# Routed feed forward in pairs of slot tiles, with a direct scatter of the last batch

## What is computed

```python
x = x + attn_a(_layernorm(x))      # 8 heads of 128, relative positions
x = x + ffn(_layernorm(x))
x = x + attn_b(_layernorm(x))      # 16 heads of 8, one shared key head, causal
x = x + ffn(_layernorm(x))
# ffn
gate_scores = softmax(x @ Wg.T)
topk_val, topk_idx = top_k(gate_scores, 2)       # shares then sum to one
for e in range(8):
    h = x @ W1[e].T + b1[e]                      # 512 columns
    a, b = split(h, 2)
    out = out + ((a * sigmoid(b)) @ Wo.T + bo) * comb[..., e:e + 1]
```

## Time and profile before

| | us |
|---|---|
| median of 3 runs | 2738.0 |
| the profiled execution, as timed | 2737.45 |
| its span in the trace | 2735.7 |
| mean granted TensorE clock (share of full speed) | 0.939 |
| first feed forward's slot tiles, first to last matmul | about 1601 to 1732 |
| end of the opening of the second attention | about 1831 |
| second feed forward, first matmul to the end | about 2544 to 2736 |

### The profile page before, as it was taken

The page is one execution under the profiler, slowest core; times in us unless marked ns, Lnnn a source line. Parts: engine busy times, 40 slices in busy tenths (PEclk is TensorE's granted clock), DMA queues, the critical chain, the costliest instruction groups (busy, mean ns, idle before and its releaser), DMA issues.

```text
span 2735.7 us, 42920 instructions
## 1 busy us (share of the span) xinstructions
PE 2468.2 (90%) x13784; PEld 1930.7 (71%) x13784; DVE 1875.9 (69%) x4952; ACT 1566.4 (57%) x3189; POOL 452.5 (17%) x827
## 2 busy tenths in 40 slices
PE   4999898999999999999999977789988988888686
PEld 3788787888888888888888865565555554554565
DVE  4677775676767778767776655578777877773464
ACT  3566665666666566666666634436657656656242
POOL 1000012000000021000110005341212223334145
PEclk7999999999999999999999989679999999999795
DMA  3665568555555566565666526310000000000264
GB/s 115 216 223 209 179 242 284 180 206 208 209 208 207 188 224 223 202 216 181 218 217 222 205 65 189 96 35 1 1 1 1 1 1 16 9 22 11 82 204 122
DMA packets 153109, 385.66 MB, mean 141 GB/s; under 512 B 17972, under 2 KB 74932, under 8 KB 152564
## 3 DMA queue, kind: packets, MB, share of 16 engines
q1 hardware_dynamic: 137562, 345.74, 36.6%
q0 software_dynamic: 12208, 35.62, 4.2%
q10 hardware_dynamic: 3120, 1.57, 0.2%
HBM read 192.02 MB, written 193.53 MB: 141 GB/s over the span
## 4 chain that ended last, share of the span: by engine, by line
PE 75%; DVE 12%; ACT 4%; issue 4%; DMA 2%; POOL 1%; another core or an unknown queue 1%; SPq 0%; ACTq 0%; DVEq 0%; POOLq 0%
PE ps L305 8%; PE ps L307 8%; PE ps L306 8%; PE ps L854 7%; PE ps L959 5%; PE ps L921 5%; PE ps L829 5%; PE ps L828 5%; PE ps L867 4%; PE ps L941 4%; PE ps L869 4%; PE ps L868 4%; DVE ps L1603 2%; ACT r_P L1177 1%; PE ps L743 1%
## 5 line engine op out<-in xcount | busy, mean ns | idle before, releaser
L1129 ACT ACTIVATE a_Ph<-ps 128x512 fp32r<-128x512 f32 x512 | 305.5, 597 | 469.1 <-PE ps L854 469.1
L1177 ACT ACTIVATE r_P<-ps 128x512 f32<-128x512 f32 (+3 forms) x768 | 330.5, 492 | 213.0 <-PE ps L941 192.8
L1520 DVE CUSTOM_DVE_ANT_0 a_sp<-ps,a_sp 128x1024 f32<-128x1024 f32 x256 | 313.2, 1223 | 180.6 <-PE ps L307 160.9
L1526 DVE TENSOR_TENSOR a_Pl<-ps,a_Ph 128x512 fp32r<-128x512 f32 x512 | 349.1, 682 | 10.0 <-ACT a_Ph L1129 10.0
L828 PE MATMUL ps<-a_fa,a_ua 128*128 128x384 f32 (+2 forms) x960 | 329.6, 355 | 27.5 <-ACT a_rt L1114 14.6
L1122 ACT ACTIVATE a_sp<-a_sp,a_nm 128x1024 f32<-128x1024 f32 x256 | 295.0, 1152 | 44.6 <-DVE a_nm L1520 43.9
L854 PE MATMUL ps<-ident,a_sp 128*128 128x128 f32 x2048 | 309.8, 274 | 0.0
L921 PE MATMUL ps<-r_K,r_Q 128*128 128x512 f32 (+3 forms) x768 | 283.9, 403 | 23.2 <-DVE r_mx L1603 13.3
L854 PEld LDWEIGHTS ps<-ident,a_sp 128*128 128x128 f32 x2048 | 252.1, 141 | 61.9 <-issue 0.8
L829 PE MATMUL ps<-a_fb,a_ub 86*128 86x384 f32 (+2 forms) x960 | 292.4, 319 | 0.0
L941 PE MATMUL ps<-r_Q,r_K 128*128 128x512 f32 (+3 forms) x768 | 257.5, 380 | 35.5 <-ACT r_P L1177 31.4
(11 more groups left out here) (239 smaller groups left out, 5129.0 us busy)
## 6 DMA issues: line engine op xcount, KB each, us to landing
scr<-a_rt SPq DMA_DIRECT2D x256, 576.0 KB
a_sp<-scr SPq DMA_DIRECT2D x256, 512.0 KB, 4.4
gsd<-m_gg SPq DMA_DIRECT2D x82, 256.0 KB
a_wc<-wsp SPq DMA_DIRECT2D x24, 512.0 KB, 5.4
m_sx<-xsd SPq DMA_DIRECT2D x38, 256.0 KB
wsp<-a_wc SPq DMA_DIRECT2D x8, 512.0 KB, 5.4
xsd<-in_q POOLq DMA_DIRECT2D x2, 1472.0 KB, 18.0
a_ub<-a_ua SPq DMA_DIRECT2D x64, 44.0 KB
```

Of the source, the lines that this page charges most:

```text
L1177: e.activation(self.P[:, pt, off:512], ps[:, bank, off:512], ACT.Exp).then_inc(S["b_exp"], 1)
L1520: e.tensor_tensor_reduce(out=w, in0=ps[:, 2:4, :].rearrange("p a n -> p (a n)"), in1=w, scale=-1.0, scalar=3e38, op0=ALU.add, op1=ALU.min, ...
L1526: e.tensor_tensor(self.Pl[:, n % 3, :], ps[:, 4 + n % 2, :], self.Ph[:, n % 3, :].bitcast(F32), ALU.subtract).then_inc(S["p_lo"], 1)
```

## The change

Slot tiles are handled in pairs. `m_mm` is now a step of up to two tiles in two neighbouring banks, with one tanh of up to 128x512 on ACT and one gated product of up to 128x512 on DVE for both. Up to the first back step the pairs use three pairs of banks in turn (0 to 5), from then on two (0 to 3). The transposes of a group of four tiles stand ahead of all pairs of the group before, in bank 6. `m_fin` uses banks 4 and 7 beside pairs and 3 and 4 after them, `m_proj` bank 5. A back step comes every 1.1 pairs (2.2 tiles), from five pairs after the first part.

The last batch has no `m_disp` on DVE: its layer norm writes into a buffer of its own, `xn8` (eight tiles), and POOL scatters from there as soon as the slots are known (new semaphores `m_slot` and `d_scat_last`); its `m_bias` goes into the middle of the rest. Its layer norm, scores, ranks and slots come one step for each pair. Of the second attention's opening the first six steps, layer norm of batch 0, stand between the pairs of the third part, in bank 6 instead of 7. Clearing the key buffer (`b_zero`) goes to the front of POOL's work, and ACT's wait for the end of the first attention comes at the first tanh.

```diff
     groups = [(part, g) for part in range(3) for g in range(PG[part])]
-    side = {0: [("b_load",)] if f == 0 else [("m_bias", 1, 2)]}
-    ln = splits(2 * f + 1)(B - 1, 7)
-    for i, it in zip((1, 2, 3, 5, 6, 8), ln):
-        side.setdefault(i, []).append(it)
-    for i, it in enumerate(gates(f, B - 1) + [None] + place(f, B - 1) + disp(f, 2) + [("m_bias", f, B - 1)]):
-        side.setdefault(10 + i, []).append(it)
+    side = {i: its for i, its in enumerate(
+        [[("ln_stats", 2 * f + 1, B - 1)], [("ln_total", 2 * f + 1, B - 1)], [("ln_scale", 2 * f + 1, B - 1, 0)],
+         [("ln_turn", 2 * f + 1, B - 1, 0, 7), ("ln_scale", 2 * f + 1, B - 1, 1)], [("ln_turn", 2 * f + 1, B - 1, 1, 7)]]
+        + [[u] for u in gates(f, B - 1) + place(f, B - 1)])}
+    side[max(side)] += disp(f, 2)
     if f == 0:
-        side.setdefault(30, []).append(("b_zero", 0))
-        side.setdefault(34, []).append(("b_prepare",))
-    last = [sum(PT[:part + 1]) - 1 for part in range(3)]
+        side[0] = [("b_load",), ("b_zero", 0)] + side[0]
+        side.setdefault(14, []).append(("b_prepare",))
+    else:
+        side.setdefault(14, []).append(("m_bias", 1, 2))
+    last = [sum(PP[:part + 1]) - 1 for part in range(3)]
     for part in range(2):
         side.setdefault(last[part], []).extend(("m_gath", f, n) for b in PARTS[part] for n in range(8 * b, 8 * b + 8))
-    back = [[u for u in (("m_sum", f, n), ("m_fin", f, n - 1, 5 + (n - 1) % 2), ("m_proj", f, n - 2, 7)) if 0 <= u[2] < NT]
-            for n in range(NT + 2)]
-    first, every = last[0] + 9, 2.6
-    p, i, nb = [("m_turn", f, 0, 0, 4), ("m_load", f, 0, 2)], 0, 0
+
+    def back(n, fin, proj):
+
+        return [u for u in (("m_sum", f, n), ("m_fin", f, n - 1, fin), ("m_proj", f, n - 2, proj)) if 0 <= u[2] < NT]
+
+    first, every = last[0] + 5, 1.1
+    p, j, nb, early = [("m_turn", f, 0, 0, 6), ("m_load", f, 0, 2)], 0, 0, list(more[:6])
     for k, (part, g) in enumerate(groups):
-        for t in range(4 * g, min(4 * g + 4, PT[part])):
-            p.append(("m_mm", f, part, t, i % 4))
-            if t % 2 or t == PT[part] - 1:
-                p.append(("m_store", f, part, t // 2))
-            if t % 4 == 1 and k + 1 < len(groups):
-                p.append(("m_turn", f, *groups[k + 1], 4))
-                if k + 3 < len(groups):
-                    p.append(("m_load", f, *groups[k + 3]))
-            p += [u for u in side.pop(i, []) if u]
-            if i >= first + every * nb:
-                p += back[nb]
+        if k + 1 < len(groups):
+            p.append(("m_turn", f, *groups[k + 1], 6))
+            if k + 3 < len(groups):
+                p.append(("m_load", f, *groups[k + 3]))
+        for n in range(2 * g, min(2 * g + 2, PP[part])):
+
+            p += [("m_mm", f, part, n, 2 * (j % 3 if j < first else j % 2)), ("m_store", f, part, n)]
+            p += side.pop(j, [])
+            if j >= first + every * nb:
+                p += back(nb, 7 - 3 * (nb % 2), 5)
                 nb += 1
-            i += 1
+            if nb > 10 and early:
+                p.append(early.pop(0))
+            j += 1
     p += [("m_gath", f, n) for n in range(8 * B - 8, 8 * B)]
-    rest = [u for its in back[nb:] for u in its]
+    rest = [u for n in range(nb, NT + 2) for u in back(n, 3 + n % 2, 5)]
+    rest.insert(len(rest) // 2, ("m_bias", f, B - 1))
     if f == 0:
         rest.append(("b_zero", 1))
-    return p + (spread(more, rest) if more else rest)
+    return p + (spread(early + more[6:], rest) if more else rest)
 
...
-    opening = splits(2)(0, 7) + first(0) + prepare(0) + chain(0)
+    opening = splits(2)(0, 6) + first(0) + prepare(0) + chain(0)
...
-        self.gg, self.sig, self.gb, self.acc, self.th, self.tl = [], [], [], [], [], []
+        self.gg, self.sig, self.gb, self.acc, self.th, self.tl, self.xn8 = [], [], [], [], [], [], []
-                self.sig.append(buf("sig", [128, 4, FH]))
+                self.sig.append(buf("sig", [128, 3, 2, FH]))
+                self.xn8.append(buf("xn", [128, 8, 128]))
...
-            for s in range(2):
-                e.wait_ge(self.d_scat[s], 16 * (NT * f + 8 * PARTS[part][-1] + 8))
+            if part == 2:
+                e.wait_ge(self.d_scat_last, 256 * (f + 1))
+            else:
+                for s in range(2):
+                    e.wait_ge(self.d_scat[s], 16 * (24 * f + 8 * PARTS[part][-1] + 8))
...
             _, f, n = u
-            i, part = NT * f + n, [n // 8 in p for p in PARTS].index(True)
-            e.wait_ge(S["m_xd"], i + 1)
+            i, part = 24 * f + n, [n // 8 in p for p in PARTS].index(True)
             if i == 0:
                 e.wait_ge(S["d_zero"], 80)
-            if f and n == 8 * PARTS[part][0]:
-                e.wait_ge(S["m_tr"], at(PG, 0, part + 1))
+            if n == 8 * PARTS[part][0]:
+                e.wait_ge(S["m_slot"], 3 * f + part + 1)
+                if f:
+                    e.wait_ge(S["m_tr"], at(PG, 0, part + 1))
+            if part == 2:
+                rows, sem = self.xn8[f][:, n - 24, :], self.d_scat_last
+                e.wait_ge(S["ln_xn"], 2 * ln_rank(2 * f + 1, B - 1) + 2)
+            else:
+                rows, sem = self.xd[:, i % 2, :], self.d_scat[i % 2]
+                e.wait_ge(S["m_xd"], i + 1)
             for k in range(2):
-                e.indirect_dma_start(self.xsd[part], bass.IndirectOffsetOnAxis(self.slot[:, k, n:n + 1], 0),
-                                     self.xd[:, i % 2, :], None).then_inc(self.d_scat[i % 2], 16)
+                e.indirect_dma_start(self.xsd[part], bass.IndirectOffsetOnAxis(self.slot[:, k, n:n + 1], 0), rows,
+                                     None).then_inc(sem, 16)
...
+
+    def rows_of(self, p, b, half):
+
+        return self.xn8[p // 2][:, 4 * half:4 * half + 4, :] if p % 2 and b == B - 1 else self.xn[:, :, :]
...
             free[bank] = S["m_xlo"], i + 1
+            _, f, part, n, bank = u
+            i, s = at(PP, f, part) + n, (at(PG, f, part) + n // 2) % 2
+            if n == 0:
+            if n % 4 == 0:
+                t, m = 2 * n, min(8, PT[part] - 2 * n)
+                e.load(self.expert[t % 16:t % 16 + m], self.mapi[0:1, part, t:t + m])
+            if n % 2 == 0:
+                e.wait_ge(S["m_xlo"], at(PG, f, part) + n // 2 + 1)
+            for t in range(2 * n, min(2 * n + 2, PT[part])):
+                hb, cs = ps[:, bank + t % 2, :], slice(128 * (t % 4), 128 * (t % 4) + 128)
+                e.wait_ge(*free[bank + t % 2])
+                k = e.snap(self.expert[t % 16], min_val=0, max_val=E - 1)
+                wh, wl = (w[:, bass.ds(k, 1), :].rearrange("p k n -> p (k n)") for w in (self.Wh, self.Wl))
+                e.matmul(hb, self.sxh[:, s, cs], wh, start=True, stop=False)
+                e.matmul(hb, self.sxh[:, s, cs], wl, start=False, stop=False)
+                m = e.matmul(hb, self.sxl[:, s, cs], wh, start=False, stop=True)
+                free[bank + t % 2] = S["m_gate"], i + 1
+            m.then_inc(S["m_mm"], 1)
...
+            _, f, part, n, bank = u
+            i, k = at(PP, f, part) + n, min(2, PT[part] - 2 * n)
+            if i == 0:
+                self.first_attention_done(e)
+            if i >= 3:
+                e.wait_ge(S["m_gate"], i - 2)
+            e.activation(self.sig[f][:, i % 3, 0:k, :], ps[:, bank:bank + k, FH:512], ACT.Tanh, scale=0.5).then_inc(S["m_sig"], 1)
...
+            xn = self.rows_of(p, b, half)
-                i = e.tensor_scalar(self.xn[:, k, :], x[:, 8 * b + m, :], mv[:, m, 0:1], rs[:, m:m + 1],
+                i = e.tensor_scalar(xn[:, k, :], x[:, 8 * b + m, :], mv[:, m, 0:1], rs[:, m:m + 1],
-                i = e.memset(self.xn[:, :, 127:128], 1.0)
+                i = e.memset(xn[:, :, 127:128], 1.0)
...
-            self.step(e.tensor_copy(self.slot[:, :, ns], self.slf[:, :, ns]))
+            e.tensor_copy(self.slot[:, :, ns], self.slf[:, :, ns]).then_inc(S["m_slot"], 1)
-            i, b = NT * f + n, n // 8
+            i, b = 24 * f + n, n // 8
+            if b == B - 1:
+                return
...
-            e.wait_ge(S["m_xd"], NT * f + 8 * b + 8)
+            if b < B - 1:
+                e.wait_ge(S["m_xd"], 24 * f + 8 * b + 8)
+            else:
+                e.wait_ge(S["ln_xn"], 2 * ln_rank(2 * f + 1, b) + 2)
...
-            _, f, part, t, bank = u
-            i, p = at(PT, f, part) + t, at(PP, f, part) + t // 2
+            _, f, part, n, bank = u
+            i, k = at(PP, f, part) + n, min(2, PT[part] - 2 * n)
-            if t % 2 == 0 and p >= 4:
-                e.wait_ge(self.d_gs[p % 4], 16 * (p // 4))
-
-            e.scalar_tensor_tensor(self.gg[f][:, p % 4, t % 2, :], self.sig[f][:, i % 4, :], 1.0, ps[:, bank, 0:FH], ALU.add,
-                                   ALU.mult).then_inc(S["m_gate"], 1)
+            if i >= 4:
+                e.wait_ge(self.d_gs[i % 4], 16 * (i // 4))
+
```

(2 more changed lines are left out.)

37 lines of the change are left out of this document (9 added, 28 removed).

## The result

The changed kernel took 2718.6 us (median of four runs, 2709.2 to 2724.8) against 2739.6 for the kernel before (2734.1 to 2744.2): a ratio of 0.9926, 95% interval 0.9897 to 0.9955. It is faster, by 21 us and not by the 48 of the forecast; 2718.6 lies near the upper end of the stated range (2667 to 2722). The profiled execution, the fastest of the four, took 2709.24 us with a span of 2707.5, 28.2 less than the span before. I cut it at the same places as before: the first slot matmul and the last one of each part. These are the stretches of the changed kernel (columns as in the earlier trace rows): part one, parts two and three, the merged opening of the second attention; then part one, parts two and three and the tail of the second feed forward.

A forecast was written before the change was run, and what follows sets the result against it. The prediction took PE's chain of waits as the bound (75% of the span PE, 12% DVE). First feed forward -26.7 and second -21.7 us, together -48.4, gave 2690 us, with a range of 2667 to 2722.

The forecast's parts named there:

- Part one: First part of each feed forward: 55 us against 68.3 and 71.0, so -13.3 and -16.0; bounds 44 and 62.
- ten matmuls at half clock: In part one, starting cold and after each of three waits, ten matmuls run at half clock: 8 us.
- Scatters and first gather: On POOL: slots within 1 us of before, 21 us of scatters, first gather 12 us earlier in each feed forward.
- Parts two and three: Of the feed forwards: +6.9 us in the first and +3.3 in the second, with 18 back steps instead of 15.
- I keep the 11 us: In parts two and three: the 11 us measured over the work at full clock were taken to stay.
- Fused products: Pair's tanh 598 ns, product 692; DVE needs 2.12 us a pair against PE's 2.42, so PE stays the bound.
- Rival D: Parts two and three: pairs starve PE, which waits for `m_gg` and drops to half clock; 2764 us, chance 0.06.
- Opening: Opening of the second attention: -20.3 us from norm waits, three back steps and bank 7; bounds -10 and -30.
- Tail: Tail of the second feed forward: three fewer row tiles of gathers, -9.0 us; bounds -4 and -14.
- B: Rival: slots 5 us later, so first gathers are not much earlier and back steps wait; 2711 us, chance 0.18.
- C: Rival: PE stays at full clock, six to ten us more saved in each feed forward; 2672 us, chance 0.12.
- E: Rival: part one's saving returns as waits for the first gather and in the merged opening; 2738 us, chance 0.04.

The follow-up runs named there:

- c3: The kernel before with the direct scatter of batch 3 alone, no other part of the change, against the kernel before: ratio 0.9924.
- a4: The changed kernel with DVE writing batch 3's rows again as before, against the kernel before: ratio 0.9995.
- c1: The changed kernel itself, run again on another chip, against the kernel before on that chip: ratio 0.9933.
- c4: The kernel before, run as a kernel of its own for its profile, against the kernel before on the same chip: ratio 1.000.
- third chip: The chip on which c1, c2, c3 and c4 were run, with the kernel before: ratios 0.9933, 0.9894, 0.9924 and 1.000.
- a2: The changed kernel with the first back step three pairs later, same spacing, against the kernel before: ratio 0.9872.
- c2: The same kernel as a2, run again beside c1 on another chip, against the kernel before: ratio 0.9894.
- a3: The changed kernel with tanh and gated product issued for each tile of a pair, against the kernel before: ratio 0.9945.
- e1: The edits of a2 and a3 together on the changed kernel, against the kernel before: ratio 0.9891.
- b3: The kernel of a2 with the second attention's first layer norm put back behind the tiles, against the kernel before: ratio 0.9877.

## Why the prediction was wrong

**Part one: right, for a reason that was too wide.** 55 us forecast, 53.2 and 53.5 measured. My sum gave the saving to everything together. c3 and a4 show that the direct scatter carries it (13.8 of c1's 15.8 us in the second feed forward, all of its 14.3 in the first), and that the pairs without it make part one longer than before. No row gave my ten matmuls at half clock after each wait. The measured clock of 0.86 and 0.84 in part one, taken as whole or half, makes 14.9 and 17.1 us at half clock and so a loss of at most 7.4 and 8.6 us, against my 8.

**Scatters and first gather: the step that began the error.** I took the slots at the same time to within 1 us, the scatters at 21 us and the first gather up to 8 us behind part one's end. Measured in the first feed forward: the first scatter 42.7 us into the stage instead of 39.5, 24.9 us from it to the first gather, part one's end 1.8 us earlier than forecast; the gather came 14.4 and 13.7 us behind that end. POOL paused twice among the scatters, 3.20 and 1.91 us, 2.96 and 1.88. Shorter pauses are there before too (0.67 and 1.42, 1.75 and 1.34), and my 1.38 us a scatter had averaged them in.

**Parts two and three: the step that failed.** "I keep the 11 us" of idle and half clock. I had the gap between part one's end and the first gather in hand and did not ask what PE's order holds in it. The first `m_fin` stands seven pairs behind part one's last; PE stood 7.1 and 8.8 us there in c1 and not at all in c4. I also counted to the gather's start and not to the landing of its data: its row is 0.99 us, and ACT's sum began 4.5 us after its start. The Trainium skill, Perfetto Trace Analysis, section "DMA Instruction — SWDGE (GPSIMD)", says that such a row ends when the descriptors are made and not when the data has moved. The trace agrees: the second gather's row ends at 2596.34, and the sum that needs it starts at 2598.56.

So the mis-sized term was 34.4 us instead of 10.2, and waiting in order was the larger part of the 24 us. That is plain on the third chip, where the same term was 33.5 us (18.1 and 15.4): PE's idle time grew by 19.2 us, 18.0 of them ahead of transposes of `m_acc`, and its busy time by 14.3. The forecast had 10.2 for all of it, so 18.0 of the 23.3 us above it are this wait. Part of the rest is busy time at a lower clock. In c4 PE's granted clock in this stretch of the second feed forward was 1.00 of 2.4 GHz. In c1 it was 0.92, and the loss is one piece at 0.50 (1.2 GHz) that begins in the wait of 8.84 us:

```profile
2562.50:2577.40 14.90, 11.94 (x59) 9.34 (x57) 6.35 (x10) 5.01 (x10) 7.79 (x9) 1.00 0.76 230
2577.40:2587.60 10.20, 3.69 (x11) 2.63 (x11) 3.18 (x6) 2.78 (x7) 7.76 (x9) 0.50 0.39 108
2587.60:2628.60 41.00, 39.19 (x236) 32.06 (x234) 27.80 (x66) 23.49 (x53) 29.40 (x31) 1.00 0.78 235
```

Late back steps (a2) took 21.2 us off part two in the two feed forwards; 10 of them came back in the tail, and the whole kernel came to 35 us under the kernel before, by its ratio, instead of 21. They shorten the wait and do not end it: for `m_acc` PE waited 18.0 us in c1's parts two and three and 10.1 in c2's.

**Fused products: costs right, worth nothing.** The pair's product, by its line:

```profile
L1436 DVE SCALAR_TENSOR_TENSOR m_gg<-m_sig,ps x88: 407/686/690, 1601.0 to 2657.8; 128x512 f32<-128x512 f32 x82, 128x256 f32<-128x256 f32 x6
```

686 ns against my 692, and in parts two and three PE waited 1.4 and 0.7 us for `m_gg`. Rival D is refuted: the clock was 0.92 and 0.91 there. The Trainium skill, TensorE: Matmul & The Clock Gate, section "A second HAM failure mode: psum-queue depth-cycling", describes a clock that goes back and forth when matmuls cycle through PSUM banks with short idle times between. In parts two and three of c1's second feed forward the trace does not show that: the clock fell once, in the wait for the first `m_acc`, and not between pairs. D's price had a slip of its own: 2.7 us against 2.42 is 0.3 us a pair and not 0.4, so 14 us and not 19. And a3 and e1 show that two single products do as well, within 0.2%.

**Opening: the sum right, its parts wrong.** -18.1 against -20.3. I gave 11.3 us to the norm's waits. PE's line for those transposes in the kernel before had 10.6 us of idle time from 1731 to 1831, and in the changed kernel it is gone from there. b3 shows that it bought nothing: with the norm back behind the tiles parts two and three of the first feed forward were 7.3 us shorter and the rest, up to the second feed forward, 6.2 us longer. The direct scatter alone shortens that rest by 9.1 us (c3 against c4, 796.2 against 805.3), with no back step fewer in it; the whole change by 23.4 (c1). What the other 14 us are made of (6 of them the norm's, by b3; three back steps fewer; bank 7) was not taken apart by runs. The two table loads took 1283 ns each, as in the earlier trace rows.

**Tail: right in size.** -8.4 against -9.0. I had reasoned by three gathers fewer. The runs tie the end of the second feed forward to its first gather instead (the third chip, above): the first gather came 8.2 us earlier in its stage than before (67.1 against 75.3), and the end followed it in 113.4 us instead of 116.3. My bound by POOL assumed gathers of 1.26 us back to back; the 64 took 100.3 us here.

**Rivals.** B (the gather not earlier by much) was closest, in mechanism and in number. Its 2711 is 27 us under the kernel before, against 28.2 in the profiles and 21 by the medians. The last scatter came 66.4 and 65.9 us into the stage, near B's 66 and 68 (its 1667 and 2612) and above my 61 and 63, and the first gathers came 6.8 and 8.2 us earlier than before, at B's own bound of 8. I had held against B that the tiles before the slots were slowed; and the cost on PE's side was missing from B as well. That its number fits is partly luck: 12 of its 27 us were the norm's, and b3 shows that the norm bought nothing. C (more goes) is refuted: part one's clock did rise, from 0.81 and 0.78 to 0.86 and 0.84, but within my 55 us, and the end lay above the forecast and not below. E (no gain) is refuted by the interval, 0.9897 to 0.9955.
